# Gates that travel with the gathered tokens, sums by two engines, and ranks for four experts at a time

## The chip, the cores and the metric

The program runs on one core of a Trainium2 chip. The engines that it uses are TensorE (PE; PEld is its weight load), VectorE (DVE), ScalarE (ACT), GpSimd (POOL) and SyncE (SP, here a DMA issuer only). A name with a q (POOLq, DVEq) is an engine's instruction queue. The metric is the time of one execution in microseconds, the median of several runs. It was 1689.83 us for the kernel before.

## The reference, cut to what matters

The model has four layers. In each, an attention stage and a feed-forward stage add to x (4096 tokens of 128 numbers). The change touches the four feed-forward stages. Three are mixtures of eight experts, and the third layer's has experts that choose their tokens.

```python
# layer 0: one expert of eight per token
weights = softmax(top_2_of(flat @ Wr));  w_top1 = weights[:, 0]
h = gelu(flat @ W1[e]);  out = w_top1 * (h @ W2[e])            # e: the token's best expert

# layer 1 (and 3, with relu and another router): two experts of eight per token
top_p, top_i = top_k(router_probs, 2);  top_p = top_p / top_p.sum()
h = gelu(x @ w1[e] + b1[e]);  expert_out = h @ w2[e] + b2[e]
out = sum over the two choices of top_p * expert_out

# layer 2: each of 16 experts takes its 512 best tokens
topk_weight, topk_idx = top_k(softmax(flat_x @ gate_w.T).T, 512)
h = gelu(xg @ Wg[e].T) * (xg @ Wu[e].T)                        # xg = flat_x[topk_idx[e]]
flat_out[topk_idx[e]] += (h @ Wd[e].T) * topk_weight[e]
out = flat_out + gelu(x @ Sg.T) * (x @ Su.T) @ Sd.T            # the shared part
```

## The kernel before

The 4096 tokens lie in on-chip memory as x [128, 32, 128]: 32 tiles of 128 tokens. Eight stages follow one another: a0, f0, a1, f1, a2, f2, a3, f3 (a for attention, f for feed-forward). Each begins with a layer norm of x into xn. Nothing is ordered by a planner: each engine has its own program in the order in which it is written, and semaphores tie the programs together.

**f0, f1 and f3** go through `route`, `experts` and `combine`.

`route` (L735) is a chain of some fifty small DVE steps. It picks each token's expert or experts, computes the two gates from one Exp on ACT, and sorts the tokens into tiles of 128 that all belong to one expert: 39 tiles in f0 (one choice), 71 in f1 and f3 (two choices). SP stores xn to the DRAM tensor d_xn (L781) as its first DMA and then loads the expert weights. In f1 and f3 a block of its own (L1661 to L1673) then turns the first biases: one PE transpose and one DVE copy.

`experts` (L915) is a software pipeline over the tiles, four tiles to a turn of the loop. For tile n:

- POOL gathers tile n+6 from d_xn (L948), then waits for y of tile n and scatters it to d_y (L952). Both are indirect DMAs, and POOL writes their descriptors, so its program is busy for each of them.
- PE computes up_proj(n+2) (L981), turns the gathered tokens of n+3 (L974) and computes down_proj(n) (L989).
- ACT copies the turned tokens (L1020), applies the activation (L1030) and copies the expert's first weights (L1015).
- DVE reads the expert's number of tile n+2 into a register (L1055), adds the first bias (L1060, 128x512) and makes y of tile n (L1075 with the second bias, L1073 a plain copy in f0). At the head of each turn it reads two more expert numbers.

`combine` (L1083) loads y back in four parts of eight token tiles. ACT multiplies the first choice by its gate (L1113, eight operations a part). In f1 and f3 DVE multiplies the second choice and adds it to x (L1131, eight operations a part). POOL adds the first choice (L1123, one 128x1024 operation a part), and DVE takes the statistics for the next layer norm (L83). In f3 SP stores each part of the output instead.

**f2** (`expert_choice`) searches a score threshold for each of the 16 experts bit by bit (L2606 to L2615; PE counts across partitions and meanwhile works on the shared part), marks the tokens above and at the threshold (L2621), ranks them by a running sum on DVE (L2622) and matmuls against a triangle (L2452 to L2457), and turns ranks into slots: two digits, one-hot tables (L2638 to L2644) and matmuls (L2463, `invert`). All this is done for 16 experts at once, up to the one-hots, which are made for four experts at a time: the first four before the expert loop, the others inside it. The loop has pairs of experts: eight pair bodies, of which the first three also prepare the next four experts each.

## Time and profile before

| what | value |
|---|---|
| median of 3 runs | 1689.83 us (1685.56 to 1692.47) |
| profiled execution, its own time | 1689.31 us |
| span of that execution | 1687.5 us, so 1.8 us lie around it |
| granted TensorE clock, mean | 0.851 of full speed |
| busy: PE, DVE, ACT, POOL | 1147.7, 793.7, 617.0, 840.8 us |
| expert loop of f0, first gather to last scatter | 110.2 to 234.7 us, 39 tiles |
| expert loop of f1 | 469.9 to 706.5 us, 71 tiles |
| expert loop of f3 | 1417.7 to 1656.3 us, 71 tiles |
| f2, marks and ranks up to the first gather | 865.8 to 890.5 us |

A time in a row is counted from the span's start. No engine is busy for more than 68% of the span: the stages are bounded by different things, so each is read by itself. In a row of instruction groups the figures behind the bar are busy time, the mean of one in ns, and how long the engine had been idle before them and what ended that. "issue" means that the engine waited for nothing that the profile shows, "remote" that it waited for a signal which the profile cannot tie to an instruction.

### The profile page before, as it was taken

The numbers are of one execution on the slowest core, as the hardware profiler recorded it, in microseconds if no ns is written. First come the engines' busy times: TensorE is split into PE (matmuls) and PEld (weight loads), VectorE is DVE, ScalarE is ACT, GpSimd is POOL, SyncE is SP. The second block draws the span as 40 slices with busy tenths as digits, with TensorE's granted clock in tenths as the row PEclk, the third lists the DMA queues.
The fourth block names the chain that finished last, engine by engine and source line by source line (L and its number), as shares of the span: only waits on it lengthen the run. The fifth ranks groups of instructions, "written<-read, shape, count | busy, mean of one in ns | idle before, by whom it ended". The sixth has DMA issues, their size and how long they took to land. (4 is left out here: it accounts for less than half of the span.)

```text
span 1687.5 us, 30101 instructions
## 1 busy us (share of the span) xinstructions
PE 1147.7 (68%) x8612; PEld 905.0 (54%) x8613; DVE 793.7 (47%) x2043; ACT 617.0 (37%) x1219; POOL 840.8 (50%) x944
## 2 busy tenths in 40 slices
PE   3547744892766777436767789937999785667771
PEld 2436742682566766425434455524788534666761
DVE  4550017467822322288873432335899536222223
ACT  2124435341344444354221122214454532444443
POOL 6136637464156555462435768835444102555554
PEclk9669877996889888868978999979999985998886
DMA  3051125000411111211212445540000013111114
GB/s 106 2 165 42 42 72 106 3 0 7 163 35 40 37 40 39 67 63 49 55 50 65 81 91 101 118 72 6 1 0 0 8 65 113 39 39 41 39 39 159
DMA packets 87352, 95.54 MB, mean 57 GB/s; under 512 B 19509, under 2 KB 66742, under 8 KB 86774
## 3 DMA queue, kind: packets, MB, share of 16 engines
q1 hardware_dynamic: 63974, 59.90, 12.0%
q0 software_dynamic: 22848, 32.67, 8.7%
q10 hardware_dynamic: 464, 2.16, 0.3%
q8 instruction: 33, 0.54, 0.1%
q14 instruction: 33, 0.27, 0.0%
HBM read 65.53 MB, written 29.16 MB: 56 GB/s over the span
## 5 line engine op out<-in xcount | busy, mean ns | idle before, releaser
L981 PE MATMUL psum<-f_xsT,f_w1e 128*128 128x128 f32 x1448 | 235.5, 315 | 152.5 <-issue 95.6
L981 PEld LDWEIGHTS psum<-f_xsT,f_w1e 128*128 128x128 f32 x1448 | 210.3, 223 | 170.0 <-issue 146.9
L952 POOL DMA_INDIRECT d_y<-f_y,f_dst x181 | 178.3, 985 | 191.7 <-DVE f_y L1075 131.4
L948 POOL DMA_INDIRECT f_xs<-d_xn,f_src x181 | 175.3, 969 | 139.3 <-SPq L944 85.0
L1060 DVE TENSOR_TENSOR f_hpre<-psum,f_b 128x512 f32<-128x512 f32 x142 | 98.2, 691 | 260.5 <-remote 93.5
L989 PE MATMUL psum<-f_w,f_hT 128*128 x1448 | 210.5, 294 | 2.8 <-ACT f_hT L1030 2.8
L989 PEld LDWEIGHTS psum<-f_w,f_hT 128*128 128x128 f32 x1448 | 196.3, 211 | 3.2 <-issue 3.2
L488 PE MATMUL psum<-ident,xn 128*128 128x128 f32 x256 | 47.8, 363 | 173.2 <-DVE xn L461 172.9
L1015 ACT COPY f_w1e<-f_w 128x512 f32 x184 | 113.7, 618 | 66.5 <-PEq L1665 30.4
L488 PEld LDWEIGHTS psum<-ident,xn 128*128 128x128 f32 x256 | 40.6, 189 | 179.4 <-ACT xn L502 173.9
L1030 ACT ACTIVATE f_hT<-f_hpre 128x512 f32<-128x512 f32 x142 | 89.5, 630 | 111.9 <-DVE f_hpre L1060 90.6
L2391 POOL DMA_INDIRECT d_acc<-f_y,f_token x64 | 102.3, 1598 | 45.5 <-DVE f_y L2676 27.9
L1020 ACT COPY f_xsT<-psum 128x128 f32<-128x128 f32 x181 | 47.7, 264 | 192.1 <-remote 115.1
L2573 ACT ACTIVATE f_g<-psum 128x512 f32<-128x512 f32 x64 | 38.2, 597 | 156.7 <-PE psum L2495 88.2
L2377 POOL DMA_INDIRECT f_xs<-d_xs,f_token x64 | 62.4, 975 | 39.3 <-issue 18.9
L2495 PE MATMUL psum<-f_xsT,f_wg 128*128 128x512 f32 x128 | 70.1, 630 | 13.6 <-DVE f_h L2666 12.2
L1075 DVE TENSOR_TENSOR f_y<-psum,f_b 128x128 f32<-128x128 f32 x142 | 40.5, 286 | 80.2 <-PE psum L989 51.9
L2666 DVE TENSOR_TENSOR f_h<-psum,f_g 128x512 f32<-128x512 f32 x64 | 44.0, 688 | 69.7 <-ACT f_g L2573 56.7
L83 DVE BATCH_NORM_STATS2 stats<-x 128x6 f32<-128x128 f32 x224 | 46.8, 278 | 48.4 <-POOL x L1123 21.9
L2495 PE MATMUL psum<-f_xsT,f_wu 128*128 128x512 f32 x128 | 68.8, 621 | 0.0
L974 PE MATMUL psum<-ident,f_xs 128*128 128x128 f32 x181 | 55.3, 305 | 17.9 <-DMA f_xs<-d_xn,f_src 17.9
L479 POOL TENSOR_SCALAR xn<-x,ln_mv,ln_rstd 128x128 f32<-128x128 f32 x56 | 47.4, 857 | 37.2 <-DVE ln_rstd L452 37.2
(462 smaller groups left out, 2356.9 us busy)
## 6 DMA issues: line engine op xcount, KB each, us to landing
f_yback<-d_y SPq DMA_DIRECT2D x20, 512.0 KB, 6.5
d_xn<-xn SPq DMA_DIRECT2D x3, 2048.0 KB, 7.6
f_w<-in_L_ffn_W SPq DMA_DIRECT2D x2, 2048.0 KB, 13.7
a_v<-in_ctx SPq DMA_DIRECT2D x4, 1024.0 KB, 7.9
f_wg<-in_WgT SPq DMA_DIRECT2D x16, 256.0 KB
f_wu<-in_WuT SPq DMA_DIRECT2D x16, 256.0 KB
f_wd<-in_WdT SPq DMA_DIRECT2D x16, 256.0 KB
f_xs<-d_xn,f_src POOLq DMA_INDIRECT x181
```

The costliest lines, as they stand in the source:

```text
L488: last = nc.tensor.transpose(k.bank[g][:, i * P:(i + 1) * P], k.xn[:, g * TPC + i, :], k.ident[:])
L948: nc.gpsimd.indirect_dma_start(xs[:, u % RX, :], None, k.d_xn, bass.IndirectOffsetOnAxis(m.src[:, n:n + 1], 0)).then_inc(gathered[u % RX], 16)
L952: nc.gpsimd.indirect_dma_start(k.d_y, bass.IndirectOffsetOnAxis(m.dst[:, n:n + 1], 0), y[:, u % RT, :], None).then_inc(scattered[u % RT], 16)
L974: nc.tensor.transpose(BT[u % 2][:, 0:P], xs[:, u % RX, :], k.ident[:]).then_inc(x_turned, 1)
L981: last = nc.tensor.matmul(BH[u % 2][:, s * P:(s + 1) * P], w1e[:, u % RT, s * P:(s + 1) * P], xsT[:, u % 2, :], start=True, stop=True)
L989: last = nc.tensor.matmul(BY[u % 2][:, 0:D], hT[:, u % RT, s, :], m.w2[:, bass.ds(e * FF + s * D, D)], start=s == 0, stop=s == HS - 1)
L1015: nc.scalar.copy(w1e[:, u % RT, :], m.w1[:, bass.ds(e * FF, FF)]).then_inc(w_copied, 1)
L1030: nc.scalar.activation(hT[:, u % RT].rearrange("p s t -> p (s t)"), src, m.act).then_inc(activated, 1)
L1060: nc.vector.tensor_tensor(hpre[:, u % 2], BH[u % 2][:].rearrange("p (s t) -> p s t", s=HS), bc(m.b1[:, bass.ds(e * HS, HS)], (P, HS, P), 2 ...
L2377: nc.gpsimd.indirect_dma_start(xs[:, e % 2, t, :], None, k.d_xs, bass.IndirectOffsetOnAxis(token[:, e, t:t + 1], 0)).then_inc(gathered[e % ...
L2391: nc.gpsimd.indirect_dma_start(k.d_acc, bass.IndirectOffsetOnAxis(token[:, e, t:t + 1], 0), y[:, e % 2, t, :], None, compute_op=ALU.add).t ...
L2495: last = nc.tensor.matmul(k.bank[bank][:], w[:, u, s * P:(s + 1) * P], xsT[:, u, :], start=True, stop=True)
```

## The change

1. **Gates travel.** A row of d_xn is 130 numbers wide instead of 128. `route` writes into the two extra columns of xn the gate of the first choice and the difference of the second to the first. The store of xn to d_xn therefore comes after the gates, and it is issued by ACT. DVE has one more step for the difference and one that marks which slots are second choices.
2. **Gates are applied in the expert loop.** DVE's `keep_gate(n+3)` copies the tile's gates out of the gathered rows (for two choices: difference times the mark, plus first). In f1 and f3 y becomes two operations, the add of the second bias and a multiplication by the gate; in f0 the copy becomes a multiplication. A gather waits for `gate_kept` where it waited for `x_turned`.
3. **`combine` only adds.** ACT's scaling and DVE's eight operations a part are gone. With two choices POOL adds one choice and then DVE the other, each as one 128x1024 operation; with one choice the parts alternate between DVE and POOL.
4. **The bias block goes.** Its transpose and copy are now the last steps of `route`.
5. **f2.** The update of thr moves to where DVE waits for PE's count. Marks, ranks and digits are made for four experts at a time: the first four before the loop, the others in its first three pair bodies.

```diff
@@ route
-    m.gate = sb("gate", [P, 2, NT])
+    m.second = sb("second", [P, m.cols])
@@ SP
-                sp.dma_start(k.d_xn[0:T, :].rearrange("(p j) d -> p j d", p=P), k.xn[:]).then_inc(xst, 16)
@@ DVE
+                of_first, to_second = k.xn_rows[:, :, D], k.xn_rows[:, :, D + 1]
+                step(TS(gate[:, 0, :], gate[:, 1, :], 1.0, None, ALU.add))
+                step(nc.vector.reciprocal(of_first, gate[:, 0, :]))
+                step(TT(gate[:, 1, :], gate[:, 1, :], of_first, ALU.mult))
+                TT(to_second, gate[:, 1, :], of_first, ALU.subtract).then_inc(gates_made, 1)
...
+                step(TS(m.second[:], tile_i[:], float(NT), None, ALU.is_ge))
...
+                if m.b1 is not None:
+                    dve.wait_ge(b1_turned, 1)
+                    step(nc.vector.tensor_copy(m.b1[:], k.bank[7][:, 0:NE * HS]))
@@ ACT
+                act.wait_ge(gates_made, 1)
+                act.dma_start(k.d_xn[0:T, :].rearrange("(p j) d -> p j d", p=P), k.xn_rows[:]).then_inc(xst, 16)
@@ experts, POOL
-                        wait(pool, x_turned, n + AHEAD - RX + 1)
+                        wait(pool, gate_kept, n + AHEAD - RX + 1)
@@ experts, DVE
+                def keep_gate(n, u):
+                    dve.wait_ge(x_turned, n + 1)
+                    wait(dve, y_ready, n - RX + 1)
+                    row, at = xs[:, u % RX], slot_gate[:, u % RX:u % RX + 1]
+                    if m.choices == 1:
+                        nc.vector.tensor_scalar(at, row[:, D:D + 1], 1.0, None, ALU.mult).then_inc(gate_kept, 1)
+                    else:
+                        nc.vector.scalar_tensor_tensor(out=at, in0=row[:, D + 1:D + 2], scalar=m.second[:, bass.ds(n, 1)],
+                                                       in1=row[:, D:D + 1], op0=ALU.mult, op1=ALU.add).then_inc(gate_kept, 1)
...
+                        if not end or u + 3 < turn:
+                            keep_gate(n + 3, u + 3)
                         if m.b1 is not None and (not end or u + 2 < turn):
                             es.append(expert_of(n + 2))
                             bias(n + 2, u + 2, es[u + 2])
                         dve.wait_ge(down, n + 1)
                         wait(dve, scattered[u % RT], 16 * (RX // RT) * i + 16 * (u // RT))
-                        if m.b2 is None:
-                            nc.vector.tensor_copy(y[:, u % RT, :], BY[u % 2][:, 0:D]).then_inc(y_ready, 1)
-                        else:
-                            nc.vector.tensor_tensor(y[:, u % RT, :], BY[u % 2][:, 0:D], m.b2[:, bass.ds(es[u] * D, D)],
-                                                    ALU.add).then_inc(y_ready, 1)
+                        src = BY[u % 2][:, 0:D]
+                        if m.b2 is not None:
+                            nc.vector.tensor_tensor(y_sum[:, u % RT, :], src, m.b2[:, bass.ds(es[u] * D, D)], ALU.add).then_inc(y_summed, 1)
+                            dve.wait_ge(y_summed, n + 1)
+                            src = y_sum[:, u % RT, :]
+                        dve.wait_ge(gate_kept, n + 1)
+                        nc.vector.tensor_scalar(y[:, u % RT, :], src, slot_gate[:, u:u + 1], None, ALU.mult).then_inc(y_ready, 1)
@@ combine
+        def add(eng, c, q):
+            eng.wait_ge(back[c][q], 16)
+            xs = flat(k.x[:, tiles(q), :])
+            return eng.tensor_tensor(xs, flat(y[:, c, q]), xs, ALU.add)
...
-                        last = nc.scalar.activation(y[:, 0, q, t, :], y[:, 0, q, t, :], ACT.Identity, scale=m.gate[:, 0, j:j + 1])
...
-                    nc.gpsimd.tensor_tensor(xs, flat(y[:, 0, q]), xs, ALU.add).then_inc(summed, 1)
+                    if by_pool(q):
+                        add(nc.gpsimd, m.choices - 1, q).then_inc(second, 1)
...
-                        last = nc.vector.scalar_tensor_tensor(out=k.x[:, j, :], in0=y[:, 1, q, t, :], scalar=m.gate[:, 1, j:j + 1],
-                                                              in1=k.x[:, j, :], op0=ALU.mult, op1=ALU.add)
...
+                        dve.wait_ge(second, q + 1)
+                    if m.choices == 2 or not by_pool(q):
+                        add(nc.vector, 0, q).then_inc(summed, 1)
@@ f2, DVE
+                    if i:
+                        step(TT(thr[:], thr[:], took[:], ALU.bitwise_or))
                     if at:
                         step(TT(nxt[:], step_i[:, at - 1, :], thr[:].broadcast_to((P, 3)), ALU.bitwise_or))
                     dve.wait_ge(counted, i + 1)
...
-                    step(TT(thr[:], thr[:], took[:], ALU.bitwise_or))
...
+                mark_greater(0)
+                mark_equal(0)
+                slot_digits(0)
...
-                                (lo_hots, hi_hots)[s % 2](group, 2 * u + s // 2)
+                            if group and u == 0 and s < 2:
+                                (mark_greater, mark_equal)[s](group)
+                            if group and u:
+                                (lo_hots, hi_hots)[s % 2](group, 1 + s // 2)
+                        if group and u == 0:
+                            slot_digits(group)
+                        if group:
+                            lo_hots(group, 3 * u)
+                            hi_hots(group, 3 * u)
                         dve.wait_ge(down, e + 1)
@@ f2, PE
-                        if group:
-                            invert(group, 2 * u)
+                        if group and u == 0:
+                            rank(group)
+                        if group and u:
+                            invert(group, 1)
```

How the order of the instructions changes is seen best on three places. The first is DVE in the expert loop of f1 (f3 is the same), one tile inside a turn; f_b is b1 for the 128x512 operation and b2 for the 128x128 one. Before:

```order
L1055 TENSOR_LOAD f_expert
L1055 ISA x2
L1060 ISA
L1060 TENSOR_TENSOR f_hpre<-psum,f_b 128x512
L1075 ISA
L1075 TENSOR_TENSOR f_y<-psum,f_b 128x128
```

And after:

```order
L1088 SCALAR_TENSOR_TENSOR f_slot_gate<-f_xs,f_second 128x1
L1072 TENSOR_LOAD f_expert
L1072 ISA x2
L1077 ISA
L1077 TENSOR_TENSOR f_hpre<-psum,f_b 128x512
L1104 ISA
L1104 TENSOR_TENSOR f_y_sum<-psum,f_b 128x128
L1108 TENSOR_SCALAR f_y<-f_y_sum,f_slot_gate 128x128
```

The gate of tile n+3 now stands ahead of the expert's number and the bias of tile n+2, and y is the last of two operations.

The second place is PE in f2, from the turned thresholds to the first invert. Before:

```order
L2447 MATMUL psum<-ident,f_thr_w 128x128
L2421 MATMUL psum<-f_sd,f_hs 128x128 x16
L2452 MATMUL psum<-f_gt,f_trim 128x512
L2453 MATMUL psum<-f_gt_sum,f_onesb 128x512
L2455 MATMUL psum<-f_eq,f_trim 128x512
L2456 MATMUL psum<-f_eq_sum,f_onesb 128x512
L2457 MATMUL psum<-f_gt_sum,f_onesb 128x512
L2463 MATMUL psum<-f_hi_val,f_lo_hot 128x64 x32
```

And after:

```order
L2458 MATMUL psum<-ident,f_thr_w 128x128
L2465 MATMUL psum<-f_gt,f_trim 128x128
L2466 MATMUL psum<-f_gt_sum,f_onesb 128x128
L2468 MATMUL psum<-f_eq,f_trim 128x128
L2469 MATMUL psum<-f_eq_sum,f_onesb 128x128
L2470 MATMUL psum<-f_gt_sum,f_onesb 128x128
L2432 MATMUL psum<-f_sd,f_hs 128x128 x16
L2478 MATMUL psum<-f_hi_val,f_lo_hot 128x64 x32
```

The ranks are a quarter as wide and stand ahead of the last shared units.

The third place is DVE in the first half of a pair body of f2, between the last of the four multiplications into f_h and y. Before:

```order
L2666 TENSOR_TENSOR f_h<-psum,f_g 128x512
L2642 TENSOR_TENSOR f_hi_hot<-f_hi_of,f_hi 128x512
L2644 TENSOR_TENSOR f_hi_val<-f_hi_hot,f_tok 128x512
L2676 TENSOR_SCALAR f_y<-psum,f_kept 128x128 x4
```

And after:

```order
L2657 SCALAR_TENSOR_TENSOR f_s<-psum,f_gt 128x128
L2659 SCALAR_TENSOR_TENSOR f_s<-psum,f_eq 128x128
L2660 TENSOR_TENSOR f_s<-f_s 128x128
L2661 TENSOR_SCALAR f_si<-f_s 128x128
L2662 TENSOR_SCALAR f_sq<-f_si 128x128
L2663 TENSOR_SCALAR f_si<-f_si 128x128
L2664 CAST f_hi<-f_sq 128x4x32
L2665 CAST f_lo<-f_si 128x4x32
L2673 TENSOR_TENSOR f_lo_hot<-f_lo_of,f_lo 128x1024
L2677 TENSOR_TENSOR f_hi_hot<-f_hi_of,f_hi 128x512
L2679 TENSOR_TENSOR f_hi_val<-f_hi_hot,f_tok 128x512
L2718 TENSOR_SCALAR f_y<-psum,f_kept 128x128 x4
```

Eight steps for the ranks' digits now stand between the last multiplication into f_h (L2701, just ahead of these rows) and y, and a whole set of one-hots instead of half of one.

## Rows read from the trace of the kernel before

**Rows 1.** Windows (f0, f1 expert loops): length, busy PE PEld DVE ACT POOL, clock, DMA, GB/s

```profile
121.00:234.00 113.00, 84.83 (x629) 81.72 (x627) 11.22 (x39) 49.35 (x108) 68.72 (x71) 0.89 0.14 41
480.00:705.00 225.00, 160.28 (x1177) 152.93 (x1175) 65.03 (x140) 99.74 (x206) 130.79 (x134) 0.90 0.13 39
```

**Rows 2.** Instruction groups of f1's expert loop, 480 to 705 us

```profile
L952 POOL DMA_INDIRECT d_y<-f_y,f_dst x70 | 69.0, 986 | 76.2 <-DVE f_y L1075 65.2 <-issue 11.0
...
L1060 DVE TENSOR_TENSOR f_hpre<-psum,f_b 128x512 f32<-128x512 f32 x69 | 47.7, 691 | 122.0 <-issue 46.9 <-remote 41.2 <-PE psum L981 25.7
```

**Rows 3.** Timeline of f1's expert loop: start, us, engine, instruction [idle before]

```profile
567.67 0.99 POOL L952 DMA_INDIRECT d_y<-f_y,f_dst  x1 [0.31 <-issue]
568.97 0.96 POOL L948 DMA_INDIRECT f_xs<-d_xn,f_src  x1 [0.30 <-issue]
...
570.99 0.29 DVE L1075 TENSOR_TENSOR f_y<-psum,f_b 128x128 f32<-128x128 f32 x1 [0.84 <-remote]
...
574.05 0.69 DVE L1060 TENSOR_TENSOR f_hpre<-psum,f_b 128x512 f32<-128x512 f32 x1 [2.77 <-issue]
574.65 0.28 DVE L1075 TENSOR_TENSOR f_y<-psum,f_b 128x128 f32<-128x128 f32 x1
...
575.29 0.69 DVE L1060 TENSOR_TENSOR f_hpre<-psum,f_b 128x512 f32<-128x512 f32 x1 [0.35 <-issue]
```

**Rows 4.** L1055, the expert's number, on DVE's queue in that loop: ns, min/median/max

```profile
L1055 DVEq TENSOR_LOAD <-f_expert x102: 298/305/441, 480.8 to 701.0; - x102
```

**Rows 5.** Timeline of f0's combine

```profile
246.61 9.45 ACT L1113 ACTIVATE f_yback<-f_yback,f_gate 128x128 f32<-128x128 f32 x32 [16.27 <-DMA f_yback<-d_y]
249.14 9.39 POOL L1123 TENSOR_TENSOR x<-f_yback,x 128x1024 f32<-128x1024 f32 x4 [14.48 <-ACT f_yback L1113]
...
258.56 1.65 DVE L83 BATCH_NORM_STATS2 stats<-x 128x6 f32<-128x128 f32 x8 [0.69 <-POOL x L1123]
```

**Rows 6.** Timeline of f1's combine

```profile
716.35 2.19 DVE L1131 SCALAR_TENSOR_TENSOR x<-f_yback,f_gate,x 128x128 f32<-128x128 f32 x8 [11.14 <-DMA f_yback<-d_y]
...
718.87 4.30 DVE L1131 SCALAR_TENSOR_TENSOR x<-f_yback,f_gate,x 128x128 f32<-128x128 f32 x8 [0.33 <-DMA f_yback<-d_y]
720.15 2.34 POOL L1123 TENSOR_TENSOR x<-f_yback,x 128x1024 f32<-128x1024 f32 x1 [13.70 <-ACT f_yback L1113]
...
734.63 1.64 DVE L83 BATCH_NORM_STATS2 stats<-x 128x6 f32<-128x128 f32 x8 [0.96 <-POOL x L1123]
```

**Rows 7.** Timeline of f2 from the last threshold step to the digits, DVE

```profile
863.89 0.16 DVE L2615 TENSOR_TENSOR f_thr<-f_thr,f_took 128x1 int32<-128x1 int32 x1
864.09 0.29 DVE L2616 TENSOR_SCALAR f_thr_w<-ones,f_thr 128x128 f32<-128x128 f32 x1
...
865.80 2.41 DVE L2621 TENSOR_TENSOR f_gt<-f_sc,f_thr_bc 128x512 bf16<-128x512 f32 x1 [0.26 <-DVE f_thr_bc L2618]
868.25 1.69 DVE L2622 TENSOR_TENSOR_SCAN f_gt_sum<-f_seg,f_gt 128x512 bf16<-128x512 f32 x1
...
878.05 0.43 DVE L2629 TENSOR_SCALAR f_si<-f_s 128x512 int32<-128x512 f32 x1
...
879.43 1.24 DVE L2632 CAST f_hi<-f_sq 128x512 bf16<-128x512 int32 x1
...
881.98 0.69 DVE L2638 TENSOR_TENSOR f_lo_hot<-f_lo_of,f_lo 128x1024 bf16<-128x1024 bf16 x1
```

**Rows 8.** Timeline of f2's first pair body, DVE

```profile
913.18 1.13 DVE L2676 TENSOR_SCALAR f_y<-psum,f_kept 128x128 f32<-128x128 f32 x4 [3.49 <-PE psum L2516]
```

**Rows 9.** Timeline from the last step of f3's route to its first gather

```profile
1415.46 0.23 DVE L871 TENSOR_TENSOR f_src<-f_pp,f_f 128x72 int32<-128x72 f32 x1
...
1416.55 0.19 DVE L1673 COPY f_b<-psum 128x32 f32<-128x32 f32 x1 [0.86 <-PE psum L1668]
...
1417.72 1.09 POOL L948 DMA_INDIRECT f_xs<-d_xn,f_src  x1 [31.52 <-SPq L944]
```

**Rows 10.** The page's DMA issues: kind, count, KB each, us from issue to landing

```profile
d_xn<-xn SPq DMA_DIRECT2D x3, 2048.0 KB, 7.6
```

152 lines of the change are left out of this document (74 added, 78 removed).

## The prediction

> **What bounds the kernel now.** No engine fills the span, so I read it stage by stage: first the windows, then the groups and the timeline of the two-choice expert loop, then the timelines of combine and of f2's ranks.
>
> The windows come first [rows 1]. In f1's loop 70 tiles pass in 225.00 us, 3.21 us a tile; in f0's, 39 in 113.00 us, 2.90 a tile. The reader is to see that f0's DVE has 11.22 us of work, f1's 65.03, while POOL and PE have nearly the same per tile. So f1's DVE work is mostly, but not wholly, hidden: it costs 0.31 us a tile.
>
> The groups and the timeline say where [rows 2, 3]. POOL waits longest for y (65.2 us before 70 scatters, 0.93 a tile), and when it does not wait, a scatter and a gather take 0.99+0.31 and 0.96+0.30 = 2.56 us. DVE in its turn waits 41.2 us for "remote" signals and 46.9 us for "issue" before the biases. In a tight tile it needs 1.24 us from bias to bias (574.05 to 575.29). That is 0.60 to y and 0.64 back, in which the expert's number is read into a register (the load alone 0.305 us [rows 4]) while y still runs for 0.28. At the head of a turn, with three such reads, y to bias takes 3.06 us, 2.4 more. Some of that may be another wait, so I take 2.0, or 0.5 a tile. DVE's cycle is so 1.24+0.5 = 1.75 us, well below POOL's 2.56. After each stall the tiles are caught up at POOL's pace, not at DVE's.
>
> **Expert loops of f1 and f3.** DVE gets two operations a tile more, and a different order. The multiplication of y is 128x128; the nearest operation took 0.29 us [rows 7], plus 0.04 to the next start (863.89+0.16 to 864.09). keep_gate is 128x1: 0.16 as the threshold step, plus 0.04. That is 0.53. keep_gate stands ahead of the value read, so the read no longer runs beside y but starts behind it: of 0.28 us that y covered I count all as exposed, 0.81. Then keep_gate waits for x_turned(n+3), which PE gives one transpose after the up_proj that bias(n+2) waited for. Queued behind that wait are the expert's number, the bias, and with them ACT's activation and PE's down_proj. I put 0.1 on it: 0.9 us a tile, a cycle of 1.75+0.9 = 2.65 us. That is just over POOL's 2.56.
>
> What that costs has two parts. The first is the longer way from up to y, which POOL feels after each stall. If 1.75 us of DVE cost 0.31 a tile between f0 and f1, 0.9 us costs 0.16, or 11 us for 71 tiles. The second is that the pace between stalls is DVE's and no longer POOL's, up to 0.09 a tile or 6 us, of which I take two thirds. Together **+15 us a stage, +30 us** for f1 and f3. From below: nothing, if PE's stalls set the pace anyway, and a y that is later by 0.9 fits into DVE's 122.0 us of idle time before the biases. From above: +25 a stage, if the exposed reads at the head also grow and the cycle is 2.9 us (0.35 over POOL's, for 71 tiles). f0: its copy becomes a multiplication of the same size and keep_gate is added to an engine busy for 11.22 of 113.00 us: nothing, to +3. The wait of the gathers moves from PE's signal to DVE's; POOL runs six tiles ahead, so it has cover, and if that is gone each gather is late by what DVE lags.
>
> A rule speaks against the multiplication. The new y reads and writes SBUF as a TENSOR_SCALAR, where the old one read PSUM. By the rows, an int32 TENSOR_SCALAR of 128x512 took 0.43 us against 0.69 for a 128x512 bias, but the 128x128 one with a scalar per partition took 0.29, no less than the 0.28 of a two-input y [rows 2, 3, 7]. The Trainium skill, "VectorE: DVE Perf Modes", Mode 2×_2P, says that a one-source op between SBUF tensors uses both read ports, and "SBUF — State Buffer", Who interferes with whom, that GpSimd is then locked out for the whole instruction. The 0.43 agrees with the mode, the 0.29 does not. By that rule each descriptor write could be held for up to 0.29 us a tile, 21 us a stage, which is the third rival below.
>
> **Combine.** ACT's scaling goes, but it ran beside the adds. What counts is DVE and POOL. In f1, eight operations of DVE take 2.19 us alone and 4.30 beside a POOL add, which takes 2.34 [rows 6]. I read this as one of the two waiting for the other. A 128x1024 add on DVE is not in the trace: the 128x512 ones take 0.69 and the 128x128 ones 0.29, so 512 more cost 0.53 (0.40 for the last 384, scaled) and it is 1.22. Strict turns then give 4 x (2.34+1.22) = 14.2 from 716.35, and the last statistics (1.64 and a gap of 0.7) end at 732.9 instead of 736.27: −3.4. f3 alike, −3.3. In f0 the adds start when the first data is there (246.61) and not after eight scalings (249.14), and DVE takes two of four: 1.22+2.34+1.22+2.34 and waits for data of 0.3 reach 254.0, statistics 256.2, against 260.21 [rows 5]: −4. Sum **−10.7**; −15 if the two engines don't hinder each other, −3 if the loads of y set the pace.
>
> **f2.** Before the loop, 865.80 to 881.98 is 16.2 us, marks, scans and digits 512 wide [rows 7]. A quarter of the width makes 2.41 to about 0.6, 1.69 to 0.5, 0.69 to 0.29, 0.43 to 0.2 and 1.24 to 0.45. Two marks and scans 2.2, three float steps 0.9, three integer steps 0.6, two casts 0.9, ten gaps 0.4, and 1.0 twice for PE: 7.0. So −9. It is at least −6, if PE's last shared units hold the first invert. The threshold update (0.16+0.04) goes into the wait for PE's count in some fourteen iterations; DVE does not always wait, so −1.5 of at most −2.8. In three pair bodies the digits (2.4 and gaps) and one set of one-hots (0.69+0.42+0.42), 4.1 us, stand before y, where DVE idled 3.49 [rows 8]: +0.6 each, +1.8; up to +2 each if the marks in the first half also come late, +6. Sum **−8.7**.
>
> **Route.** Two steps more per stage, each 0.16 to 0.29 with its gap: +1.4 in three stages. The bias block goes, its copy stays: in f3 the copy (0.19, and 0.04 before it) then follows L871's end at 1415.69, and the gather the copy by the 0.98 that it does now, at 1416.9 instead of 1417.72 [rows 9]: −0.8. In f1 that lies beside other work, I count nothing. The store of xn starts later, behind the gates, and takes 7.6 us [rows 10]; the some forty steps after the gates cover it, and if they did not, each stage would be some us late. +0.6.
>
> **Sum.** 1689.31 + 30 − 10.7 − 8.7 + 0.6 = 1700.5, the profiled execution's time, 0.5 us under the median of the runs shown. I forecast **1700 us**. A difference under 0.5%, 8.4 us, is what a measurement of this kernel can't tell from none: 1681.4 to 1698.3 is "same".
>
> **The rivals.**
>
> *First, the loops absorb it.* DVE is idle for 160 of 225 us, and its waits are for PE's stalls ("issue", "remote"), which the change does not lengthen. For it: DVE's work of 0.93 us a tile against f0's 0.29 costs only 0.31. Against it: POOL waits for y alone, and y moves later. Then +4 a stage remains: 1689.3+8−18.8 = 1678.5. Faster.
>
> *Second, half is absorbed.* The value read still runs beside keep_gate and y: 0.53 us a tile and a cycle of 2.3, under POOL's 2.56. 0.53/1.75 x 0.31 = 0.09, 7 us a stage: 1689.3+14−18.8 = 1684.5. Same.
>
> *Third, DVE or its port sets the loop.* The cycle is 2.9 us, or the multiplication holds POOL's descriptor writing: +21 to +25 a stage. It decides as soon as a tile of POOL takes over 2.8 us without waiting for y, or a tile of DVE does. 1689.3+46−18.8 = 1716.5. Slower.
>
> *Fourth, f2 gives nothing*, its one-hots and inverts being late instead: −8.7 becomes 0, 1709 with the forecast's loops.
>
> **Chances.** Forecast 0.40, with its own range 1690 to 1710; loops absorb 0.22; half 0.13; DVE or port 0.19; f2 gives nothing 0.06. Of the forecast's part 0.12 lies below 1698.3. Faster is the first rival and 0.02 of the second, 0.24; same 0.12+0.11 = 0.23; slower the rest, 0.53. The range runs from 1672, which is the first rival with combine's −15 and part of the threshold's −2.8, to 1720, the third with 3 for f0.
>
> **What would show it.** In the profile after: DVE's bias to bias in a tight tile 2.1 us and more; POOL's wait for y over 65.2 us and f1's 225 us of loop at 240; "DVE gate_kept" as a releaser of gathers only if DVE lags by tiles. Combine of f1 from its first add to the last statistics at 16.5 us, the DVE adds being 1.2 or 3.6 us long. f2's first one-hot 7 us after the turned thresholds, the three pairs at 31 us. The forecast is wrong if a tight tile stays under 1.9 us, or if POOL's own time for a tile rises.

## The result

| | before | changed |
|---|---|---|
| median, 12 runs each | 1689.53 us (1684.97 to 1697.24) | 1682.63 us (1675.92 to 1685.51) |
| ratio, 95% interval | | 0.9956 (0.9938 to 0.9974) |
| span of the profiled execution | 1687.5 us | 1683.8 us |

The changed kernel is 0.4% faster, and I had forecast 1700 us, slower. That is not the whole result. The record does not name the chip of this measurement. The kernel before was timed again on five chips that it does name. It took 1700.69 us on one (runs e1 to e4, where the changed kernel itself was not run) and some 1552 us on the four others, and on those four the changed kernel was slower in every comparison:

| chip | before | changed | ratio, 95% interval |
|---|---|---|---|
| A (runs e5 to e8) | 1552.07 | 1567.8 | 1.0100 (1.0076 to 1.0124) |
| B (e9 to e12) | 1551.93 | 1569.79 | 1.0113 (1.0084 to 1.0141) |
| C (e13 to e16) | 1551.42 | 1564.08 | 1.0093 (1.0061 to 1.0125) |
| D (e17, e18) | 1552.1 | 1566.29 | 1.0100 (1.0083 to 1.0117) |

I call a chip slow where before takes 1690 to 1700 us, and fast where it takes 1552 us. Whether the first measurement and e1 to e4 used one slow chip or two is not known. The difference does not lie in single runs: in one measurement all runs of a kernel agree within about 1%, or 1.3% on a slow chip. Each chip was measured in one session only, so the difference may also lie in the state that a chip was in at the time.

### The profile page after: what moved, and what is told of

It reads as the page before. It is cut to its first block and busy times, and to the rows that moved or that the text cites. A ratio compares the mean times of both kernels' runs of the same rounds, so it can differ in the third digit from the quotient of the medians.

```text
span 1683.8 us, 30812 instructions
## 1 busy us (share of the span) xinstructions
PE 1139.0 (68%) x8627; PEld 891.0 (53%) x8628; DVE 873.4 (52%) x2354; ACT 584.2 (35%) x1123; POOL 835.5 (50%) x942
## 5 line engine op out<-in xcount | busy, mean ns | idle before, releaser
L998 PE MATMUL psum<-f_xsT,f_w1e 128*128 128x128 f32 x1448 | 222.3, 301 | 174.7 <-ACT f_xsT L1037 115.0
L998 PEld LDWEIGHTS psum<-f_xsT,f_w1e 128*128 128x128 f32 x1448 | 194.6, 209 | 198.8 <-ACT f_w1e L1032 109.5
L1006 PE MATMUL psum<-f_w,f_hT 128*128 x1448 | 200.8, 284 | 3.5 <-ACT f_hT L1047 3.5
L1006 PEld LDWEIGHTS psum<-f_w,f_hT 128*128 128x128 f32 x1448 | 186.1, 201 | 3.8 <-issue 3.8
L1088 DVE SCALAR_TENSOR_TENSOR f_slot_gate<-f_xs,f_second 128x1 f32<-128x1 f32 x142 | 33.6, 237 | 120.2 <-issue 51.6
L2701 DVE TENSOR_TENSOR f_h<-psum,f_g 128x512 f32<-128x512 f32 x64 | 44.0, 688 | 71.0 <-ACT f_g L2592 59.3
L1104 DVE TENSOR_TENSOR f_y_sum<-psum,f_b 128x128 f32<-128x128 f32 x142 | 40.3, 283 | 53.2 <-PE psum L1006 51.5
## 6 DMA issues: line engine op xcount, KB each, us to landing
d_xn<-xn ACTq DMA_DIRECT2D x3, 2080.0 KB, 11.7
```

The lines of the kernel that those rows point to most:

```text
L998: last = nc.tensor.matmul(BH[u % 2][:, s * P:(s + 1) * P], w1e[:, u % RT, s * P:(s + 1) * P], xsT[:, u % 2, :], start=True, stop=True)
L1006: last = nc.tensor.matmul(BY[u % 2][:, 0:D], hT[:, u % RT, s, :], m.w2[:, bass.ds(e * FF + s * D, D)], start=s == 0, stop=s == HS - 1)
```

## The profile after

The columns of this table are lengths in us from one timeline each: from the first gather of a stage to the end of its last scatter, and what lies between these. The third and fourth columns are of a fast chip (the kernel before with one wait more, which cost nothing there, e6; the changed kernel, e5).

| stretch | before | changed | fast: before+wait | fast: changed |
|---|---|---|---|---|
| start to f0's first gather | 110.17 | 111.26 | 110.18 | 109.67 |
| f0 expert loop | 124.48 | 127.55 | 101.83 | 103.01 |
| f0 combine to a1's layer norm | 27.25 | 23.58 | 27.05 | 23.66 |
| a1 | 154.11 | 155.10 | 154.52 | 154.85 |
| f1 route | 53.93 | 55.63 | 55.46 | 55.46 |
| **f1 expert loop** | 236.52 | 239.16 | 185.84 | 201.76 |
| f1 combine to a2's layer norm | 31.23 | 29.64 | 31.00 | 29.54 |
| a2 | 46.84 | 46.85 | 46.86 | 46.84 |
| f2, layer norm to first gather | 106.01 | 97.61 | 101.61 | 97.57 |
| f2 expert loop | 232.88 | 233.92 | 220.40 | 219.07 |
| f2's last scatter to a3's layer norm | 14.29 | 13.80 | 13.91 | 14.49 |
| a3 | 189.86 | 191.11 | 188.18 | 191.46 |
| f3 route | 90.15 | 90.10 | 90.15 | 90.15 |
| **f3 expert loop** | 238.61 | 239.96 | 186.35 | 200.30 |
| f3, from the last scatter | 31.16 | 28.50 | 31.12 | 28.28 |

Read the two bold lines across. On the chip of the first result the gates' work in the two-choice loops cost 2.6 and 1.4 us where I had put 15 each. On the fast chip it cost 15.9 and 14.0.

The windows of f1's loop show two regimes. The columns are those of [rows 1]. First the changed kernel as first profiled:

```profile
483.00:708.00 225.00, 153.84 (x1180) 143.16 (x1180) 98.68 (x274) 98.97 (x207) 129.02 (x132) 0.96 0.13 39
```

Then the changed kernel on fast chip A:

```profile
457.00:640.00 183.00, 144.86 (x1156) 135.11 (x1154) 94.59 (x269) 95.47 (x204) 128.08 (x131) 0.99 0.16 47
```

And the kernel before with one wait, on the same fast chip:

```profile
457.00:640.00 183.00, 150.11 (x1188) 138.85 (x1188) 62.32 (x141) 99.99 (x209) 132.96 (x136) 0.99 0.16 49
```

PE's granted clock was 0.90 before [rows 1], 0.96 after on the first chip, and 0.99 on the fast chip. What costs the kernel before its time on the first chip stands in its timeline, here where three tiles follow one another closely:

```profile
555.68 1.06 PE L981 MATMUL psum<-f_xsT,f_w1e 128*128 128x128 f32 x8
...
556.58 0.27 PE L974 MATMUL psum<-ident,f_xs 128*128 128x128 f32 x1
...
559.80 0.69 DVE L1060 TENSOR_TENSOR f_hpre<-psum,f_b 128x512 f32<-128x512 f32 x1 [3.52 <-remote]
560.48 0.27 ACT L1020 COPY f_xsT<-psum 128x128 f32<-128x128 f32 x1 [3.27 <-remote]
...
560.85 2.05 PE L981 MATMUL psum<-f_xsT,f_w1e 128*128 128x128 f32 x8 [3.10 <-issue]
```

By its record PE has turned the tokens at 556.85, but ACT, which waits for nothing else, copies them at 560.48, 3.6 us late. PE's next work waits for that copy. When it comes, the same eight matmuls take 2.05 us instead of 1.06: the clock is granted at 0.5, 1.2 GHz, after 3.1 us of idle. In f1's loop the clock falls ten times, 10 to 27 us apart. ACT's copy has 13 "remote" waits of over 1 us there and comes 1.8 to 4.8 us after the recorded end of the transpose. The ends of matmuls in a profile are modelled, so it is also possible that PE itself ended later than its record says; no run here tells the two apart. The groups of ACT's copy and DVE's bias in f1's loop show the sum. Before, in 485 to 700 us:

```profile
L1020 ACT COPY f_xsT<-psum 128x128 f32<-128x128 f32 x66 | 17.4, 263 | 58.5 <-remote 36.8 <-PE psum L974 20.2 <-issue 1.4
```

And the changed kernel on the first chip, the same window:

```profile
L1077 DVE TENSOR_TENSOR f_hpre<-psum,f_b 128x512 f32<-128x512 f32 x66 | 45.6, 692 | 45.0 <-issue 45.0
L1104 DVE TENSOR_TENSOR f_y_sum<-psum,f_b 128x128 f32<-128x128 f32 x65 | 18.4, 283 | 27.1 <-PE psum L1006 26.1 <-remote 0.9
L1037 ACT COPY f_xsT<-psum 128x128 f32<-128x128 f32 x65 | 16.9, 260 | 15.5 <-remote 8.3 <-PE psum L991 7.2
L1088 DVE SCALAR_TENSOR_TENSOR f_slot_gate<-f_xs,f_second 128x1 f32<-128x1 f32 x65 | 15.5, 238 | 46.7 <-issue 23.9 <-DVE f_y L1108 8.9 <-remote 8.5
```

ACT's "remote" idle time fell from 36.8 to 8.3 us. DVE's bias no longer has any (41.2 in [rows 2]); keep_gate, which now waits ahead of it, has 8.5. So on this chip the longer cycle of DVE replaced another loss of about the same size. It did not come on top.

DVE's cycle itself comes close to the forecast. Fast chip A, changed kernel, DVE:

```profile
540.21 0.69 DVE L1077 TENSOR_TENSOR f_hpre<-psum,f_b 128x512 f32<-128x512 f32 x1 [0.70 <-issue]
540.82 0.28 DVE L1104 TENSOR_TENSOR f_y_sum<-psum,f_b 128x128 f32<-128x128 f32 x1
541.14 0.29 DVE L1108 TENSOR_SCALAR f_y<-f_y_sum,f_slot_gate 128x128 f32<-128x128 f32 x1
541.63 0.22 DVE L1088 SCALAR_TENSOR_TENSOR f_slot_gate<-f_xs,f_second 128x1 f32<-128x1 f32 x1 [0.21 <-PE psum L991]
542.54 0.69 DVE L1077 TENSOR_TENSOR f_hpre<-psum,f_b 128x512 f32<-128x512 f32 x1 [0.69 <-issue]
...
545.46 0.22 DVE L1088 SCALAR_TENSOR_TENSOR f_slot_gate<-f_xs,f_second 128x1 f32<-128x1 f32 x1 [1.71 <-issue]
546.38 0.69 DVE L1077 TENSOR_TENSOR f_hpre<-psum,f_b 128x512 f32<-128x512 f32 x1 [0.70 <-PE psum L998]
```

Bias to bias takes 2.33 us inside a turn (540.21 to 542.54; 1.24 in [rows 3]) and 3.84 over a turn's head (542.54 to 546.38). That is (3 x 2.33 + 3.84)/4 = 2.71 us a tile, against my 2.65 and POOL's 2.56. From the 10th to the 60th scatter of this loop POOL's pace is 2.72 us a tile, and 2.57 in e6. The sum hit partly by luck: the tight tile is 2.33 and not 1.24+0.9 = 2.14, and the turn's head adds 0.38 and not 0.5. The gap of 0.70 ahead of each bias is the read of the expert's number, which nothing hides any more.

Combine in f1, to be set beside [rows 6]:

```profile
722.19 2.34 POOL L1133 TENSOR_TENSOR x<-f_yback,x 128x1024 f32<-128x1024 f32 x1 [9.91 <-DMA f_yback<-d_y]
724.57 1.22 DVE L1133 TENSOR_TENSOR x<-f_yback,x 128x1024 f32<-128x1024 f32 x1 [13.82 <-POOL x L1133]
724.73 8.89 POOL L1133 TENSOR_TENSOR x<-f_yback,x 128x1024 f32<-128x1024 f32 x3 [0.20 <-DMA f_yback<-d_y]
728.02 3.34 DVE L1133 TENSOR_TENSOR x<-f_yback,x 128x1024 f32<-128x1024 f32 x1 [2.23 <-POOL x L1133]
...
736.18 1.20 DVE L1133 TENSOR_TENSOR x<-f_yback,x 128x1024 f32<-128x1024 f32 x1
737.31 3.18 DVE L85 BATCH_NORM_STATS2 stats<-x 128x6 f32<-128x128 f32 x16
```

The DVE add takes 1.20 us with POOL idle (736.18) and 1.22, as worked out, where it begins 0.16 us ahead of POOL's add (724.57); where POOL's add began first it takes 3.34. Three POOL adds take 8.89 instead of 7.0. The two engines thus do take turns. From the first add to the last statistics it is 18.3 us where before took 19.9 and I had 16.5. The end is not POOL's last add (733.62) but DVE's own queue: its adds and the statistics of two parts stand one behind the other.

f2, to be set beside [rows 7]:

```profile
865.45 0.16 DVE L2636 TENSOR_TENSOR f_thr<-f_thr,f_took 128x1 int32<-128x1 int32 x1
865.52 1.26 POOL L2358 TENSOR_TENSOR f_hs<-f_us,f_gs 128x512 f32<-128x512 f32 x1 [0.94 <-ACT f_us L2565]
865.64 1.23 DVE L2637 TENSOR_SCALAR f_thr_w<-ones,f_thr 128x128 f32<-128x128 f32 x1
867.29 0.17 DVE L2639 COPY f_thr_bc<-psum 128x16 f32<-128x16 f32 x1 [0.42 <-PE psum L2458]
867.50 0.72 DVE L2645 TENSOR_TENSOR f_gt<-f_sc,f_thr_bc 128x128 bf16<-128x128 f32 x1
868.25 1.17 DVE L2646 TENSOR_TENSOR_SCAN f_gt_sum<-f_seg,f_gt 128x128 bf16<-128x128 f32 x1
...
873.54 0.69 DVE L2673 TENSOR_TENSOR f_lo_hot<-f_lo_of,f_lo 128x1024 bf16<-128x1024 bf16 x1
...
877.08 0.43 DVE L2679 TENSOR_TENSOR f_hi_val<-f_hi_hot,f_tok 128x512 bf16<-128x512 bf16 x1
879.55 0.69 DVE L2673 TENSOR_TENSOR f_lo_hot<-f_lo_of,f_lo 128x1024 bf16<-128x1024 bf16 x1 [2.05 <-PE psum L2478]
```

From the first mark to the first one-hot it is 6.0 us instead of 16.2 (I had 7.0). Then the third one-hot waits 2.05 us for PE, whose inverts stand behind the last shared units, as the change's order has them. So 8.4 of the 10.2 us are left at the first gather. That is one profile of each kernel; f2 up to its first gather took 92.8 to 98.4 us in the five profiles of the changed kernel. One row is odd: thr_w, a multiplication of SBUF data by one number per partition, takes 1.23 us here, while POOL is in a 1.26 us multiplication (865.52), against 0.29 in [rows 7]. I come back to it below.

## The experiments

All times are set against the kernel before on the same chip.

**e1 and e2: more DVE work in the loops of before (slow chip, before 1700.69 us).**

```diff
+                        if m.b1 is not None:
+                            for r in range(K):              # e1: K = 1, e2: K = 2
+                                nc.vector.memset(pad[:, K * u + r, :], 0.0)
                         dve.wait_ge(down, n + 1)
```

> The kernel before, with one idle DVE operation more per tile in the expert loops of f1 and f3 (a memset of 128x512, some 0.6 us) between the bias of tile n+2 and y of tile n. It computes nothing that is used. Theory (the two-choice loop of before has a pace of its own of 3.2 us a tile, set by late signals of PE and the half clock that follows them; a slower DVE evens PE's work out and takes these losses away instead of adding to them): the two loops stay within 2 us of 236.5 and 238.6 us, their granted clock rises from 0.90 over 0.92, and the whole is within 4 us of before. Rival (the terms of my prediction: 0.31 us of pace per 1.75 us of DVE work, in proportion): 0.6 us a tile cost 0.11 us, 8 us a stage, +15 us in all.

> The same with two such operations a tile, some 1.2 us, which brings DVE's own cycle to about 3.0 us a tile (1.75 before plus 1.2), near the 3.2 us that a tile takes. Theory: DVE begins to set the pace here; the clock is 0.95 or more, no signal of PE comes 3 us late, and the two loops grow by 0 to 10 us each. Rival (in proportion): 1.2 us cost 0.21 us a tile, 15 us a stage, +30 us in all, and the clock stays at 0.90.

Measured: e1 1704.67 us, 1.0033 (1.0005 to 1.0061); e2 1719.25 us, 1.0114 (1.0084 to 1.0144). The two loops take 244.8 and 244.0 us in e1, 251.3 and 251.0 in e2. Unchanged loops take 241.8 and 241.6 on this chip (e4). These are single profiles, and f0's loop, which has the same code in e1, e2 and e4, took 121.9, 122.5 and 128.8 us, so a difference of 3 us between loops is not clear of noise. The clock did not rise. This is the window 485 to 700 us of e1's loop:

```profile
485.00:700.00 215.00, 149.40 (x1049) 143.10 (x1049) 85.21 (x187) 90.42 (x185) 121.52 (x125) 0.87 0.13 38
```

And ACT's copy of the turned tokens in it:

```profile
L1021 ACT COPY f_xsT<-psum 128x128 f32<-128x128 f32 x62 | 16.3, 263 | 68.7 <-remote 44.7 <-PE psum L975 23.9
```

My theory of that time, that any slower DVE evens PE out, fell: the late signals stayed (44.7 us). The proportional rival had the size too large for both: 3.0 and 2.4 us a loop instead of 8 in e1, 9.6 and 9.4 instead of 15 in e2.

**e3, e10, e15: the place of keep_gate.**

```diff
-                        if not end or u + 3 < turn:
-                            keep_gate(n + 3, u + 3)
                         if m.b1 is not None and (not end or u + 2 < turn):
                             es.append(expert_of(n + 2))
                             bias(n + 2, u + 2, es[u + 2])
+                        if not end or u + 3 < turn:
+                            keep_gate(n + 3, u + 3)
```

> The changed kernel with keep_gate(n+3) behind the bias of tile n+2 instead of ahead of the read of the expert's number. The read then runs beside y again and the bias is not queued behind x_turned. Theory (the changed loop is paced by the ring bias, activation, up and down projection, y, keep, read, bias): the ring is 0.2 to 0.5 us shorter a tile; the loops are 0 to 8 us shorter each than the changed kernel's 239.2 and 240.0, but PE packs tighter again and its late signals come back, clock under 0.96. Rival (the order of keep_gate was never a cost): the DVE cycle and both loops are as in the changed kernel within 1 us.

Measured on the slow chip: 1709.29 us, 1.0053 (1.0023 to 1.0082), slower than before; the loops take 252.3 and 252.7 us, 11 more than unchanged ones there, at a clock of 0.86. The same window:

```profile
485.00:700.00 215.00, 149.45 (x1040) 143.24 (x1039) 83.51 (x246) 90.20 (x183) 119.54 (x122) 0.86 0.13 38
```

ACT's copy in it:

```profile
L1037 ACT COPY f_xsT<-psum 128x128 f32<-128x128 f32 x61 | 16.2, 265 | 61.9 <-remote 43.4 <-PE psum L991 16.1 <-PE psum L998 1.2
```

The late signals are back in full (43.4 us against 8.3 in the changed kernel's first profile). That the late signals would return, at a clock under 0.96, I had foreseen; but I had expected the loops to be shorter or equal.

> keep_gate behind the bias, on the same chip as the kernel with it ahead. Theory: on a slow chip the loops are 6 to 12 us longer each than with keep_gate ahead and the clock is under 0.90; on a fast chip they are 2 to 8 us shorter each, since there only DVE's cycle counts and the read of the expert's number runs beside y again. Rival (the order does not matter, e3 was the chip): within 2 us of e9 on either.

> keep_gate behind the bias. Theory: on a slow chip the loops take 250 us, some 10 more each than e13, with a clock under 0.90; on a fast chip 188 us, 13 less each than e13. Rival: equal to e13 on a slow chip.

Measured on fast chips: 1539.82 us, 0.9920 (0.9893 to 0.9947), and 1540.7 us, 0.9939 (0.9918 to 0.9959), against 1.0113 and 1.0093 of the changed order on the same chips. The loops take 189.1 and 187.7 us in e10 (188.9 and 187.6 in e15), 12.7 and 13.9 less than with keep_gate ahead on chip B (e9). e10's theory for a fast chip had the sign right and the size too small (2 to 8 us a loop); e15's 188 us held. DVE in e10, with one POOL row:

```profile
539.89 0.69 DVE L1077 TENSOR_TENSOR f_hpre<-psum,f_b 128x512 f32<-128x512 f32 x1 [2.29 <-issue]
540.44 0.97 POOL L964 DMA_INDIRECT f_xs<-d_xn,f_src  x1 [0.30 <-issue]
540.50 0.21 DVE L1088 SCALAR_TENSOR_TENSOR f_slot_gate<-f_xs,f_second 128x1 f32<-128x1 f32 x1
540.62 0.28 DVE L1104 TENSOR_TENSOR f_y_sum<-psum,f_b 128x128 f32<-128x128 f32 x1
540.94 0.50 DVE L1108 TENSOR_SCALAR f_y<-f_y_sum,f_slot_gate 128x128 f32<-128x128 f32 x1
541.84 0.69 DVE L1077 TENSOR_TENSOR f_hpre<-psum,f_b 128x512 f32<-128x512 f32 x1 [0.40 <-issue]
```

Bias to bias is 1.95 us, 0.38 less than with keep_gate ahead, for the same operations: the idle 0.21 has gone, and 0.40 of the 0.70 is left, since the read runs beside y. The pace from the 10th to the 60th scatter is 2.57 us again, POOL's. The multiplication took 0.50 us here instead of 0.29; the part on the rivals comes back to that. Swapping two lines is so worth 1.9% of the whole on one chip (0.9920 against 1.0113).

**e4: f2's part alone, on the kernel before (slow chip).**

> The kernel before with the f2 part of the change alone (threshold update, ranks for four experts at a time). Theory (the stages' lengths in the two profiles add up): f2 from its layer norm to the first gather is 8.4 us shorter, its loop 1 us longer, the whole 1681 to 1683 us, and the gates' part alone is worth about 0. Rival: f2's gain is partly given back in the loop, and the change's gain comes from combine; then 1685 us or more.

Measured: 1688.73 us, 0.9933 (0.9902 to 0.9965), a gain of 12 us in the median, with an interval from 6 to 17. In the profile f2 up to the first gather takes 92.7 us, 13 less than in the first profile of the kernel before, and the loop 234.9 (232.9 there). The first measurement's 8 us stand within the interval. The absolute time that I had expected came from the first measurement, where the kernel before was 11 us faster.

**e5, e9, e13, e17: the changed kernel again.**

> The changed kernel as it is, to stand beside the other runs of this chip. Theory (with keep_gate ahead of the bias, the bias waits for x_turned and for the read, so that PE is fed evenly, its signals are not late and its clock does not fall; this order is what makes the gates' work free): its two-choice loops take 239 to 240 us again with a clock of 0.95 or more, 12 us less each than with keep_gate behind the bias (252), and the whole is 0.3 to 0.6% faster than before. Rival (the 12 us are a difference between chips): here they take 248 us or more, the clock is under 0.92, and the whole is not faster than before.

> The changed kernel again, to stand beside its own reordering on one chip. Theory (two kinds of chips: on one, PE's signals come late and its clock halves in the loops, and the even pace of this order avoids that; on the other nothing is late and DVE's longer cycle is paid in full): if the kernel before takes 1690 us or more here, the two-choice loops take 239 to 245 us at a clock of 0.95, and the whole is 0 to 0.6% faster than before; if before takes some 1550 us, the loops take 201 us and the whole is 1.0% slower. Rival (the first result was chance): a slow chip and loops of 248 us or more.

> The changed kernel, for a chip of the slow kind (before at 1690 us or more). Theory (the even feeding of PE): two-choice loops 239 to 245 us, clock 0.94 to 0.97, the whole 0 to 0.6% faster than before. Rival: the loops 248 us or more and the whole slower. On a chip of the fast kind: loops 201 us, 1.0% slower, as in e5 and e9.

> The changed kernel, once more for a chip of the slow kind. Theory (the place of keep_gate feeds PE evenly): there its two-choice loops take 239 to 245 us, clock 0.94 to 0.97, the whole 0 to 0.6% faster than before, against 252 us and 0.86 with keep_gate behind the bias. Rival (the first profile was chance): 248 us or more. On a fast chip: 201 us, 1.0% slower.

Measured: the table at the top, four fast chips, 1.0% slower on each; two-choice loops between 200.3 and 203.5 us. Neither side of e5 had foreseen that. None of the four is a slow chip.

**e6, e14, e18: one wait more in before, no work.**

```diff
+                        if m.b1 is not None and (not end or u + 3 < turn):
+                            dve.wait_ge(x_turned, n + 4)
                         if m.b1 is not None and (not end or u + 2 < turn):
                             es.append(expert_of(n + 2))
```

> The kernel before, with one wait more in the two-choice loops: before the read of the expert's number and the bias of tile n+2 DVE waits for x_turned(n+3). No work is added. Theory (it is the later bias that evens PE out): the clock of these loops rises to 0.94 or more, 'remote' idle time of DVE falls from 41 us to under 15 us, and the loops take 225 to 236 us, since the 0.8 us a tile of the gates' work are not there: up to 2% faster than before. Rival (a wait alone only delays): the loops are as before or up to 5 us longer each, clock 0.90.

> The kernel before with the wait for x_turned(n+3) ahead of the read and the bias of tile n+2, and no work added. Theory: on a slow chip the later bias evens PE out, the clock rises over 0.93, 'remote' idle time of DVE falls under 20 us, and the loops are up to 10 us shorter than before. Rival (it takes DVE's longer cycle too, the wait alone does nothing): the loops as before within 3 us, clock 0.90. On a fast chip: as before, as in e6.

> The kernel before with the wait for x_turned(n+3) ahead of the read and the bias. Theory: on a slow chip clock over 0.93 and loops up to 10 us shorter than before. Rival: within 3 us of before, clock 0.90. On a fast chip: as before.

Measured on three fast chips: 0.9994 (0.9973 to 1.0014), 1.0008 (0.9993 to 1.0023), 0.9998 (0.9985 to 1.0011). There the wait itself costs nothing, and the loops run at POOL's pace: 185.8 to 186.5 us, 2.62 a tile with the start of the pipeline and 2.57 from the 10th to the 60th scatter. e6's POOL in such a loop:

```profile
540.48 0.99 POOL L952 DMA_INDIRECT d_y<-f_y,f_dst  x1 [0.30 <-issue]
541.78 0.97 POOL L948 DMA_INDIRECT f_xs<-d_xn,f_src  x1 [0.30 <-issue]
543.05 0.99 POOL L952 DMA_INDIRECT d_y<-f_y,f_dst  x1 [0.30 <-issue]
```

What the wait does on a slow chip stays open; none of the three fell on one.

**e7: the same wait and a DVE operation ahead of the bias (fast chip).**

```diff
+                        if m.b1 is not None and (not end or u + 3 < turn):
+                            dve.wait_ge(x_turned, n + 4)
+                            nc.vector.memset(pad[:, u, :], 0.0)
```

> The same wait and behind it one idle DVE operation (memset of 128x512, 0.6 us) ahead of the read. The same DVE work as in e1, whose loops took 244 us, only ahead of the bias and not behind it. Theory: the loops take 228 to 240 us with a clock of 0.95, so less than in e1 with the same work. Rival (the amount of DVE work counts, not its place): 244 us or more, clock under 0.90.

Measured: 1550.68 us, 0.9998 (0.9979 to 1.0018); loops 185.7 and 186.3 us. DVE is busy for 92.0 us of a 168 us window, 32 more than in e6, at no cost: the pace is still POOL's 2.57. So the 15 us of the changed kernel are no price of DVE work as such. What does cost time is a DVE cycle over POOL's, 2.71 us in e5. What it would do on a slow chip it does not say.

**e8: the change without f2's part (fast chip).**

> The changed kernel with the f2 stage of before. Theory: f2's part is worth 8 to 11 us (e4 against before on its chip: 0.67%), so the rest of the change (gates, combine, bias block) is worth -3 to +4 us: 0.9980 to 1.0025 of before. In the profile the two-choice loops cost +2 to +3 us each, the three combines give back 8 us. Rival: f2's part and the gates' part hinder each other and this kernel alone is 0.5% faster than before.

Measured: 1585.57 us, 1.0222 (1.0196 to 1.0248), 17.8 us over e5, more than f2's part is worth. In its one profile f3's loop took 209.6 us instead of 200.3 at a clock of 0.96, and f2 up to the gather 108.5. Its pace there is 2.89 us a tile where e5 has 2.72, and the clock fell to half five times inside the loop, in e5's not once before its last 2 us. I cannot explain the 9 us in a stage whose code is that of e5, and leave it open. Both sides of the expectation were wrong.

**e11, e12, e16: the second bias by PE.**

```diff
+                    if m.b2 is not None:
+                        nc.tensor.matmul(BY[u % 2][:, 0:D], k.ones[0:1, :], m.b2[0:1, bass.ds(e * D, D)], start=True, stop=False)
...
-                    es = [expert_of(RX * i), expert_of(RX * i + 1)] if m.b1 is not None else []
...
-                            nc.vector.tensor_tensor(y_sum[:, u % RT, :], src, m.b2[:, bass.ds(es[u] * D, D)], ALU.add).then_inc(y_summed, 1)
```

> The changed kernel with the second bias added by PE (one matmul of a row of ones against the expert's row of b2, first in the down projection), so that y is a single multiplication from PSUM by the gate, and DVE reads no expert's numbers at the head of a turn. keep_gate stays ahead. DVE loses one operation a tile (0.33 us) and two reads a turn (0.35 us a tile): cycle 2.7 to 2.0. Theory: on a fast chip the loops take 186 to 189 us, POOL's pace, 13 us less each, and the whole is 0.7 to 1.0% faster than before; on a slow chip they take 228 to 245 us. Rival (the added matmul is paid): nothing gained on either.

> The same with keep_gate behind the bias. Theory: on a fast chip as e11 within 2 us, both at POOL's pace; on a slow chip slower than e11 by 3 us or more a loop. Rival (the order does not matter): equal on a slow chip too.

> The second bias by PE, keep_gate ahead of the bias. PE has 16 us more work in each two-choice loop and DVE less. Theory: on a slow chip PE's work is what its late signals come from, so the loops are 5 to 20 us longer than e13's; on a fast chip 192 us as in e11. Rival (DVE's cycle counts on a slow chip too): 225 to 238 us.

Measured on fast chips: e11 1545.64 us, 0.9962 (0.9947 to 0.9976); e12 1544.92 us, 0.9966 (0.9945 to 0.9986); e16 1544.94 us, 0.9961 (0.9940 to 0.9982). The loops take 191 to 193 us, so 9 to 10 less than the changed kernel's, not the 13 that I expected. PE is now busy nearly all the time, as two windows show, e11 in f1 and then in f3:

```profile
456.00:629.00 173.00, 172.84 (x1284) 152.74 (x1284) 79.11 (x202) 95.38 (x203) 127.16 (x130) 0.98 0.17 49
1336.00:1511.00 175.00, 174.92 (x1286) 154.19 (x1287) 79.30 (x202) 95.70 (x203) 127.18 (x131) 0.97 0.17 49
```

Even so it is POOL that gives the pace in the middle of the loop, again in e11's f1:

```profile
542.07 0.99 POOL L968 DMA_INDIRECT d_y<-f_y,f_dst  x1 [0.30 <-issue]
543.36 0.97 POOL L964 DMA_INDIRECT f_xs<-d_xn,f_src  x1 [0.30 <-issue]
544.63 0.99 POOL L968 DMA_INDIRECT d_y<-f_y,f_dst  x1 [0.30 <-issue]
```

From the 10th to the 60th scatter a tile takes 2.57 us, as in e6, so the added matmuls (two instructions a tile) cost nothing there. What is lost lies at the ends of the loop: the first scatter comes 15.6 us after the first gather instead of 11.8 in e6, and the whole loop is 5.5 us longer than e6's. With POOL the bound, the order of keep_gate no longer matters (e11 against e12), as e12's theory had it. This is faster than before, but e10, two lines swapped, is faster still on the same chip (1539.82 us) and is the best version for fast chips. For a slow chip nothing is decided between e4, f2's part alone (0.9933), and the changed kernel (0.9956): they come from two measurements, and their intervals overlap.

## Why the prediction was wrong

**The forecast and where it stood.** I said 1700 us and measured was 1682.63. Every part that I had put at other than nothing moved the way I had said, but the sum did not. Against the first profile, part by part:

| term | forecast | first chip | fast chip |
|---|---|---|---|
| f1 and f3 loops | +30 | +4.0 | +29.9 |
| f0 loop | 0 (to +3) | +3.1 | +1.2 |
| combine, three stages | −10.7 | −7.9 | −7.7 |
| f2, all | −8.7 | −7.9 | −4.8 |
| route and the rest | +0.6 | +5.0 | +3.1 |

The last column is e5 less e6, one profile each, and sums to 21.6; the timed ratios say 1.0% of 1552, 15 us. Single profiles differ by some us in a1, a3 and the threshold search. (a3 alone took 187.8 and 191.5 us in profiles of the same kernel.) The f0 loop's +3.1 also lies within the spread of its unchanged code on slow chips (121.9 to 128.8 us), and of "route and the rest" 2.2 of the 5.0 us (on the fast chip all of the 3.1) lie in a1 and a3, which the change does not touch. The store of xn took 11.7 us instead of the 7.6 that I had carried over [rows 10]; f0's first gather came at 109.67 us against 110.18 on the fast chip, so nothing shows that it was waited for.

**The step that failed** is the first part of the loops' cost: "If 1.75 us of DVE cost 0.31 a tile between f0 and f1, 0.9 us costs 0.16, or 11 us for 71 tiles", with the second, "that the pace between stalls is DVE's and no longer POOL's", on top. Both take PE's stalls as given and put DVE's cycle beside them; so did the first rival, where I called them stalls "which the change does not lengthen". On the first chip they were no constant. In f1's loop of the kernel before, PE's signals come up to 4.8 us late by its records, and the clock falls to half ten times; in the changed kernel most of this is gone (8.3 us of "remote" at ACT's copy instead of 36.8, clock 0.96 instead of 0.90). So the two loops cost 4.0 us together and not 30. The profile showed both before the change, and I had written the "remote" waits down, but as a constant. The 0.31 us was also misread. It set 39 tiles against a window of 113 us that is shorter than their loop; whole loops give 3.19 us a tile for f0 (124.48 for 39) and 3.33 for f1 (236.52 for 71), 0.14 apart. And that was a price from within the stalls: on fast chips f0's loop takes 2.61 us a tile (101.83 for 39) and f1's 2.62 (185.84 for 71). e6 and e7 show that without stalls DVE work costs nothing up to POOL's pace, and in e1, with stalls, a memset of 0.49 us between bias and y cost some 0.04 us a tile.

**What was right.** DVE's cycle: 2.65 us forecast, 2.71 measured. Its mechanism, the read that nothing hides any more and the wait ahead of the bias: moving keep_gate behind the bias gives 12.7 and 13.9 us back a loop on fast chips (e9 and e10, same chip). The price of 15 us a loop came out on the four fast chips, but by luck in its parts. Of it 11 us were for a longer way after each stall, and there are no stalls there (no "remote" wait in the profiles of e5, e6, e10 and e11). What e5's f1 loop pays against e6 is the pace, 0.15 us a tile or some 10 us, for which I had put 4, and some 5 us at its start and end. That the sum is right there does not make the forecast of the measured chip right: the trace that I argued from showed a chip of the other kind.

**Is it the place of keep_gate that did it on the slow chip?** The evidence is the changed kernel's first profile (loops 239.2 and 240.0 us, clock 0.96) against e3 (252.3 and 252.7, clock 0.86), the same operations in another order. They come from two measurements, whose unchanged loops differ by 3 to 5 us (e4 against before). So some 8 to 10 us a loop belong to the order, if the measurements differ in nothing else. The timed ratios agree: 0.9956 and 1.0053, each against the kernel before in its own measurement, are 16 us apart. That is suggested but not shown, since no run has both orders on one slow chip, and e8 shows that the same loop can differ by 9 us for a reason that I don't know. Tight feeding of PE is argued only: PE ran without a gap for over 6 us ten times in f1's loop of the kernel before and twice in the changed kernel's, but eight of the 13 late copies there followed a stretch of only 2.1 or 2.2 us. Why the signals are late, and why only on some chips, is open too.

**The rivals.** The second (1684.5) came nearest to the time of the first measurement, but by the wrong way, for the read does not run beside keep_gate. The first (the loops absorb it, 1678.5) came nearest in the loops, 4 us a stage against 2.6 and 1.4, though its reason, stalls that stay as they are and hide the work, is not what happened. The signs that I had named did not settle it: a tight tile took 2.33 us, as the forecast had it, while POOL waited for y in f1's loop for 64.4 us of 225, not for more than 65.2.

The third had DVE set the loop: on fast chips it does, at 2.71 us a tile and not 2.9. Its other half, that the multiplication holds POOL's descriptor writing, did not happen: POOL's scatters took 985 ns before and 985 after. It is the multiplication that waited. In e10's f1 loop 38 of the 71 took 0.34 to 0.53 us. Over the two-choice loops of e3, e10, e15 and the changed kernel's five profiles, all 133 that began 0.50 to 0.70 us after the start of a POOL indirect DMA ended 1.00 to 1.02 us after that start (in the rows of e10, 540.94+0.50 against 540.44). Of the 837 that began clear of that stretch, before or after it, 817 took 0.29 or 0.30 us and none over 0.36. In the changed order hardly any fell there (1 of 71 in f1 of the first profile). The Trainium skill, "SBUF — State Buffer", Who interferes with whom, has whichever of the two issues first hold the shared ports and the other wait. The waits of the multiplication agree with that, and so does thr_w, which took 1.23 us beside a POOL multiplication that had begun 0.12 us earlier and 0.29 alone. The section's "for the whole instruction" does not fit POOL's indirect DMAs here: multiplications that began in the first 0.47 us of one were not held.

**Combine and f2.** In f1's combine the sum forgot that DVE has to make statistics between its adds: 4 x 1.63 and four adds are 11.4 us of DVE, and its waits for POOL are nearly another 5 (2.23 before the second add, 2.1 and 0.6 within the second and third), so DVE ends last. −3.4 became −1.6. f2 from its first mark to its first one-hot came within 1 us.
